# Turning the edge features and the one-hot tile by transpose-mode matmuls in the second edge pass of a graph network

## The reference, cut to what matters

```python
edge_index = stack([src, dst])
x = layernorm(x + L0(x, edge_index))               # mean and max over neighbours, two batch norms
x = layernorm(x + L1(x, edge_index, edge_attr))    # attention over edges

# L1, 8 heads of 12:
Q, K, V = x @ Wq + bq, x @ Wk + bk, x @ Wv + bv
E = edge_attr @ We + be                             # 206250 x 96
score = exp(clip(sum_over_head(K[src] * Q[dst] / sqrt(12) * E), -5, 5))
out = segment_sum(V[src] * score, dst) / (segment_sum(score, dst) + 1e-6)
```

## Time and profile before

| | |
|---|---|
| median of three runs | 4223.53 us |
| the profiled execution | 4223.99 us, its span 4222.3 us |
| busy: PE, POOL, DVE, ACT | 3928.9, 3080.3, 2301.6, 1500.0 us |
| first edge pass, about | 20 to 2042 us |
| node stage, about | 2042 to 2118 us |
| second edge pass, about | 2118 to 4180 us |
| last stage, about | 4180 to 4222 us |

### The profile page before, as it was taken

How to read it: one execution, slowest core, us unless ns; L and a number is a source line. 1 busy time by engine, 2 the same in 40 slices (tenths; PEclk the granted TensorE clock), 3 DMA queues, 4 the chain that set the end, 5 groups by cost and what they waited for, 6 DMA issues and landing times.

```text
span 4222.3 us, 109736 instructions
## 1 busy us (share of the span) xinstructions
PE 3928.9 (93%) x32024; PEld 3450.1 (82%) x32024; DVE 2301.6 (55%) x5891; ACT 1500.0 (36%) x4201; POOL 3080.3 (73%) x3253
## 2 busy tenths in 40 slices
PE   7988888888888888888899999999999999999996
PEld 6777777777777777777689999999999999999995
DVE  6555555555555555555645555555555555555556
ACT  3333333333333333333433333333333333333334
POOL 7777777777777777777367777777777777777774
PEclk9999999999999999999899999999999999999997
DMA  3111111111111111111144444444444444444442
GB/s 92 40 40 39 40 39 40 39 39 40 39 40 39 40 39 40 39 40 39 49 119 117 116 116 117 117 115 116 116 117 115 116 116 116 116 116 116 116 116 72
DMA packets 208677, 330.89 MB, mean 78 GB/s; under 512 B 72877, under 2 KB 156520, under 8 KB 208648
## 3 DMA queue, kind: packets, MB, share of 16 engines
q0 software_dynamic: 129040, 238.05, 23.6%
q1 hardware_dynamic: 79608, 92.48, 7.0%
HBM read 323.08 MB, written 7.22 MB: 78 GB/s over the span
## 4 chain that ended last, share of the span: by engine, by line
PE 52%; POOL 24%; issue 19%; DMA 2%; DVE 2%; POOLq 1%; ACT 0%; SPq 0%; DVEq 0%; ACTq 0%
POOL kvg L413 24%; PE bank L1221 10%; PE bank L1199 10%; PE bank L1207 10%; PE bank L1216 9%; PE bank L1238 8%; DMA kvg<-in_x_dram,idx 2%; PE bank L1230 2%; PE bank L1041 1%; PE bank L1052 1%; PE bank L1101 1%; PE bank L1084 0%; PE bank L1184 0%; PE bank L1043 0%; POOLq L408 0%
## 5 line engine op out<-in xcount | busy, mean ns | idle before, releaser
L413 POOL DMA_INDIRECT kvg<-kv_table,idx x1613 | 1524.9, 945 | 536.9 <-issue 484.5
L413 POOL DMA_INDIRECT kvg<-in_x_dram,idx x1613 | 1527.4, 947 | 497.1 <-issue 488.5
L678 DVE TENSOR_TENSOR_SCAN scan<-keepC,scan,bank 96x512 f32<-96x512 bf16 x404 | 515.4, 1276 | 495.2 <-PE bank L1052 491.0
L1041 PE MATMUL bank<-ident,kvg 128*96 128x128 f32 x3232 | 451.3, 283 | 226.3 <-DMA kvg<-in_x_dram,idx 216.2
L1041 PEld LDWEIGHTS bank<-ident,kvg 128*96 128x96 f32 x3232 | 366.5, 164 | 290.3 <-DMA kvg<-in_x_dram,idx 217.0
L941 DVE COPY qwin<-bank 64x96 f32<-64x96 f32 x404 | 100.5, 249 | 833.6 <-PE bank L1238 816.8
L1101 PEld LDWEIGHTS bank<-S,scanE 128*96 128x96 f32 x3232 | 338.9, 165 | 217.3 <-issue 214.0
L492 ACT COPY scanE<-bank 128x384 f32<-128x384 f32 x404 | 193.2, 478 | 751.3 <-PE bank L1093 749.4
L1221 PE MATMUL bank<-qwin,scan 64*128 64x96 f32 x3232 | 456.2, 282 | 0.0
L565 ACT COPY eaC<-bank 96x512 f32<-96x512 f32 x404 | 234.7, 581 | 618.1 <-PE bank L1199 610.4
L1199 PE MATMUL bank<-ident,ea 128*96 128x128 f32 x3232 | 450.3, 283 | 0.4 <-ACT stage L528 0.4
(11 more groups left out here) (155 smaller groups left out, 5365.2 us busy)
## 6 DMA issues: line engine op xcount, KB each, us to landing
ea<-in_edge_attr_dram SPq DMA_DIRECT2D x402, 192.0 KB
kvg<-in_x_dram,idx POOLq DMA_INDIRECT x1613, 2.5
kvg<-kv_table,idx POOLq DMA_INDIRECT x1613
kv_table<-stage SPq DMA_DIRECT2D x6, 672.0 KB, 3.3
xN<-in_x_dram SPq DMA_DIRECT2D x6, 336.0 KB, 3.1
out_dram<-xN SPq DMA_DIRECT2D x6, 336.0 KB
src_all<-in_src_groups_dram SPq DMA_DIRECT2D x1, 804.0 KB
stage<-in_dst_groups_dram SPq DMA_DIRECT2D x1, 804.0 KB
```

The lines of the kernel that those rows point to most:

```text
L413: pool.indirect_dma_start(out=to[:, r, j, :], out_offset=None, in_=table, in_offset=bass.IndirectOffsetOnAxis(ap=idx[:, r, j:j + 1], axis= ...
L678: dve.tensor_tensor_scan(out=scan[:, r % 2, :], data0=keepC[:, r % 2, :], data1=bank[2 + r % 2][0:D, :], initial=scan[:, (r + 1) % 2, GE - ...
L1041: pe.matmul(bank[0][0:D, j:GE:J], xg[:, r, j, 0:D], ident[:, :], start=True, stop=True)
```

## The change

In `transposes(r)` of the second pass the two ordinary products with the identity become transposes in PE's transpose mode. The operands, the banks, the waits and the signals are the same. Nothing else changes.

```diff
                     for j in range(J):
-                        last = pe.matmul(bank[0][0:D, j * P:(j + 1) * P], ea[:, r, j, :], ident[:, :], start=True,
-                                         stop=True)
+                        last = pe.transpose(bank[0][0:D, j * P:(j + 1) * P], ea[:, r, j, :], ident[:, :])
                     last.then_inc(s_Te, 1)
...
                     for j in range(J):
-                        last = pe.matmul(bank[1][0:W, j * P:(j + 1) * P], S[:, r % R, j, :], ident[:, :], start=True,
-                                         stop=True)
+                        last = pe.transpose(bank[1][0:W, j * P:(j + 1) * P], S[:, r % R, j, :], ident[:, :])
                     last.then_inc(s_T, 1)
```

## The result

The changed kernel takes 5247.96 us (median of 4 runs, 5243.27 to 5248.52) where the kernel before took 4224.08 beside it: a ratio of 1.2423, interval [1.2402, 1.2445]. It is slower by 1024 us, where 33 us less were forecast. One run of the kernel before, beside e5 to e8, took 4801.67 us at a mean granted clock of 0.738; it has no trace, its cause is open, and the ratios leave it out.

What follows compares the result with a forecast made beforehand. PE was taken to bound the second pass at 5.08 us a group, with gathers a floor at 5.00. From 4223.99 us, 28.5 (gathers' pace) and 5.0 (PE's end lag) come off: 4190.5 us, range 4186 to 4196.

Steps and rivals of the forecast that it cites:

- The bound: Second pass: PE bounds it at 5.08 us a group; after the change POOL's gathers do, at 5.00.
- the saving: Second pass on PE: eight of sixteen matmul instructions a group go, 0.87 us, leaving 4.21 us a group.
- what is late next: Second pass: DVE waits for each gather to land; its product comes 3.15 us after the group's last gather starts.
- the sum: Whole kernel: 4223.99 us less 33.5 (28.5 from the gathers' pace, 5.0 from PE's lag at the end) is 4190.5.
- 1.9: Second pass on PE: estimated longest stretch without an ordinary product, 1.1 us of transposes plus 0.8 idle.
- the 1.23 that held: First pass: a 1.23 us stretch of transposes and idle time on PE, with the granted clock at 1.00.
- the 3.15 that fell: Node stage: 3.15 us with transposes alone on PE, busy 1.48 us, after which the clock went to 0.50.
- Clock (slower): Rival, second pass: clock falls and stays low for much of it; 7.96 us a group, about 5390 throughout; chance 0.08.
- short falls are hidden: Argument against the clock rival: half-clock time up to a share of 0.21 of the second pass hides under the gathers.
- a share f of the pass: Part of the second pass at half clock; PE's mean is 4.21 + 3.75 f us a group, slower than today from 0.23.

Runs made afterwards that it cites:

- e5: Kernel before the change, with POOL held up once by clearing a dead tile after twelve groups of the second pass: 4231.58 us, ratio 1.0018.
- e8: Changed kernel with three extra ordinary products a group between the two turnings, run in five rounds: 4193.69 us, ratio 0.9929.
- e9: Kernel before, turning by products but only two of a group's four blocks, with 24 extra products in the third turn: 5251.39 us, ratio 1.2431.
- e3: Changed kernel with six extra transposes of the identity a group between the two turnings: 4195.96 us, ratio 0.9927.
- e6: Changed kernel with three of a group's four gathers, so that PE never waits for one: 5271.28 us, ratio 1.2479.
- e10: Changed kernel with three of a group's four gathers and 24 extra products in the third turn: 3879.52 us, ratio 0.9184.
- e7: Changed kernel with all its gathers and one burst of 24 extra products in group 32: 5208.99 us, ratio 1.2331.
- e4: Changed kernel with only the edge features turned by transposes, the one-hot by ordinary products as before: 4199.3 us, ratio 0.9938.
- the fillers: Changed kernel with useless work between the two turnings of each group: three products (4192.02 us, again 4193.69) or six transposes (4195.96 us).
- e11: Changed kernel with three extra products a group between the turnings and POOL held up once after twelve groups: 4199.77 us, ratio 0.9954.
- e12: Changed kernel with three extra products a group standing apart and POOL held up once after twelve groups: 5972.42 us, ratio 1.4138.

## Why the prediction was wrong

**The bound, the saving, what is late next**: right. PE's group went to 4.17 us (4.21 said). The gathers became the bound at 1.2506 us each (1.2498 said), and DVE's product waited for their DMA, as said. Where the clock holds, the sum comes out: e8, which the gathers bound, has a median of 4193.69 us where 4190.5 was forecast.

**The step that failed** is "1.9 lies between, nearer to the 1.23 that held than to the 3.15 that fell, so I take 1.00 for the pass". What came was 0.50 from 2161.37 on and 7.67 us a group on PE, against gathers of 5.00. It failed in three ways. It compared stretches without an ordinary product, and e9 fell with products alone while e3 held with 14 transposes a group: the kind of instruction was the wrong thing to count. It took the wait at its mean of 0.8 us, and the landings scatter: 6.27 and 3.64 us around 5.00, so that one wait was 1.93 and the stretch without an ordinary product 3.10 us (from 2157.49 to 0.53 behind 2160.06), beside the 3.15 that fell. And it took the clock of the first pass, which has waits too and stays at 1.00, as a sign for a loop made up of other lines.

**The rival that came true** was priced well and held unlikely. "Clock (slower)" said 7.96 us a group and about 5390 us for the whole pass; it was 7.67 and 5248. The 0.29 us come from both kinds of lines: by starts the turnings take 0.88 + 0.99 = 1.87 us at half clock (1.10 x 1.81 = 1.99 said), the rest 5.80 (5.97 said). That is 404 x 0.29 = 117 us; the nine groups before the fall are 9 x 2.59 = 23 more, together 140 of the 142 by which 5390 was too high. What held its chance down to 0.08 was "short falls are hidden", with a share f of the pass as if that were free to take any value. It is not. A PE that is quicker than the gathers waits, the wait throws the clock down, at half clock PE is slower than the gathers and never waits again, and its loop does not lift the clock (e6, e10, e7). So f is near 0 or near 1. In the kernel before, the fall of e5 is short (6.83 us); the change takes away, with the eight instructions, what made it short.

**Open.** Why the place of the work decides was not tested by itself. Nor is a long stretch always enough: the six long instructions that the kernel issues in the pass's third group to keep the clock up took 4.85 us in e10 (2138.08) and did not lift it, in the changed kernel 4.53 us (2129.98, clock 1.00 from 2134.07) and did; the burst of 48 lifted it in e7 and in e10. And e4 and the fillers change two things, how much PE waits and what it does at half clock; e5, e11 and e12 show the second, the first is shown only by e10, which has no waits. It is not shown either which waits throw the clock down: e9 fell after 0.80, 0.43 and 0.62 us, and e7 had held through 1.00, 0.81 and 0.49 in three groups running. Some of the longer waits of e7 (0.93, 0.96 and 1.20 us, ended at 2418.26, 2438.28 and 2458.43) lie four groups, one turn, apart; why the gathers land late there is open.

## What to carry to other kernels

Before you make TensorE faster than what feeds it, price its loop at half clock against the feeder: if it is then slower than the feeder (7.67 against 5.00 us here), one late transfer can cost the whole stage and not a few microseconds. Test the loop with one long wait and look at whether the granted clock comes back, since a busy PE says nothing on it. A saving that ends on the floor of another engine can be kept by spending the slack on work of no use beside the turning work (30 us gained here).

## What the runs showed of the hardware

One and the same loop without waits ran at 7.67 us a group through the whole pass (e6, clock 0.50 for 3163 us) or at 4.18 for 1659 us at 1.00 (e10), by the clock at which it began. fp32 transposes hold the clock and bring it back (e3), and one needs one instruction where a product of the same tile needs two (L1199: 1616 in place of 3232). Gathers that start every 1.25 us landed so that DVE took up their groups 6.27 and 3.64 us apart. Waits of 0.80, 0.43 and 0.62 us in successive groups came before a fall in e9, while in e4 waits of up to 0.80 us and in e7 waits of up to 1.00 us were followed by none.
